# A four-layer transformer on one core: a repeating slot schedule replaced by one place for every operation of every batch

## What is computed

```python
x = x + tanh(g_xattn[0]) * xattn0(layernorm(x), ctx)   # 16 heads of 64, causal mask, softmax
x = x + tanh(g_ffn[0])   * ffn0(layernorm(x))          # ternary weights, 8-bit rows, silu gate
x = x + tanh(g_xattn[1]) * xattn1(layernorm(x), ctx)   # 16 heads of 8, mask
x = x + tanh(g_ffn[1])   * moe(layernorm(x))           # 8 experts, top 2, capacity 269 rows
x = x + tanh(g_xattn[2]) * xattn2(layernorm(x), ctx)   # one head, padding mask
x = x + tanh(g_ffn[2])   * ffn2(layernorm(x))          # gelu, layernorm inside, ternary weights
x = x + tanh(g_xattn[3]) * xattn3(layernorm(x), ctx)   # 16 heads of 8, biases
x = x + tanh(g_ffn[3])   * ffn3(layernorm(x))          # rmsnorm, relu squared, ternary weights
```

## Time and profile before

| | us |
|---|---|
| median of 3 runs | 485.5 (485.41 to 485.64) |
| span of the profiled execution | 482.6 |
| what lies around the span (485.5 - 482.6) | 2.9 |
| PE busy in the span | 388.5 (81%) |
| DVE busy | 287.2 (60%) |
| ACT busy | 263.1 (55%) |
| POOL busy | 180.6 (37%) |

### The profile page before, as it was taken

How to read it: one execution, slowest core, us unless ns; L and a number is a source line. 1 busy time by engine, 2 the same in 40 slices (tenths; PEclk the granted TensorE clock), 3 DMA queues, 4 the chain that set the end, 5 groups by cost and what they waited for, 6 DMA issues and landing times.

```text
span 482.6 us, 9945 instructions
## 1 busy us (share of the span) xinstructions
PE 388.5 (81%) x3550; PEld 281.1 (58%) x3564; DVE 287.2 (60%) x859; ACT 263.1 (55%) x781; POOL 180.6 (37%) x294
## 2 busy tenths in 40 slices
PE   3866999999997898999962999427778999889633
PEld 0645777767876665665541899315555666665522
DVE  3151575688687878665562121643546566898884
ACT  3234757676675778877631433422464766555532
POOL 3186334333424311355363000388726442221120
PEclk9597999999999999999985899855699999999955
DMA  8990000000000030000003241111000000000001
GB/s 338 394 381 6 1 2 1 1 2 2 2 1 1 1 133 1 1 13 18 20 22 93 59 130 36 45 33 27 7 0 1 3 1 1 2 2 3 3 0 43
DMA packets 7135, 22.11 MB, mean 46 GB/s; under 512 B 1215, under 2 KB 3503, under 8 KB 6575
## 3 DMA queue, kind: packets, MB, share of 16 engines
q1 hardware_dynamic: 6063, 19.38, 11.1%
q0 software_dynamic: 1024, 2.10, 1.5%
HBM read 14.60 MB, written 6.88 MB: 44 GB/s over the span
## 4 chain that ended last, share of the span: by engine, by line
PE 61%; ACT 11%; POOL 9%; DVE 7%; issue 7%; DMA 3%; SPq 0%; POOLq 0%; another core or an unknown queue 0%; DVEq 0%; ACTq 0%
PE bank L839 6%; PE bank L908 6%; PE bank L866 5%; ACT prob L565 5%; PE bank L1031 4%; PE bank L1022 3%; POOL moe_rows L488 3%; PE bank L822 3%; PE bank L854 3%; PE bank L903 3%; PE bank L917 3%; PE bank L810 3%; DVE mx L1236 3%; PE bank L888 2%; PE bank L975 2%
## 5 line engine op out<-in xcount | busy, mean ns | idle before, releaser
L565 ACT ACTIVATE prob<-bank,mx 128x128 f32<-128x128 f32 x256 | 82.3, 384 | 23.4 <-DVE mx L1236 23.2
L1236 DVE TENSOR_REDUCE mx<-bank 128x4 f32<-128x512 f32 x96 | 63.9, 682 | 41.0 <-PE bank L839 21.5
L468 POOL TENSOR_TENSOR prob<-prob,rden 128x512 f32<-128x512 f32 x32 | 33.2, 1039 | 69.2 <-DVE rden L1258 69.2
L550 ACT ACTIVATE probT<-bank 128x512 f32<-128x512 f32 x64 | 39.5, 617 | 29.9 <-PE bank L866 29.8
L866 PE MATMUL bank<-pack,prob 128*128 128x128 f32 x256 | 41.5, 286 | 7.6 <-POOL prob L468 4.6
L443 POOL TENSOR_TENSOR rstd<-rstd,minus_half 128x1 f32<-128x1 f32 x72 | 41.3, 573 | 6.0
L441 POOL TENSOR_SCALAR rstd<-mv 128x1 f32<-128x1 f32 x64 | 12.4, 193 | 83.0 <-DVE mv L1211 79.6
L866 PEld LDWEIGHTS bank<-pack,prob 128*128 128x128 f32 x256 | 28.7, 143 | 16.4 <-POOL prob L468 6.6
L488 POOL DMA_INDIRECT moe_rows<-yrows_d,row_of x16 | 16.0, 999 | 52.2 <-DMA yrows_d<-o_n 48.3
L462 POOL TENSOR_SCALAR xn<-pack,mv,rstd 128x128 f32<-128x128 f32 x32 | 25.9, 811 | 5.9 <-POOL rstd L443 5.4
L565 ACT ACTIVATION_READ_ACCUMULATOR prob<-bank,mx 128x1 f32 x128 | 27.9, 218 | 0.0
(11 more groups left out here) (233 smaller groups left out, 965.2 us busy)
## 6 DMA issues: line engine op xcount, KB each, us to landing
yrows_d<-moe_rows SPq DMA_DIRECT2D x2, 1510.0 KB, 21.2
pack<-pack_d SPq DMA_DIRECT2D x1, 2112.0 KB, 15.7
expert<-experts_d SPq DMA_DIRECT2D x4, 514.0 KB, 8.5
pack<-experts_d SPq DMA_DIRECT2D x4, 514.0 KB, 5.1
pack<-pack_d SPq DMA_DIRECT2D x1, 2048.0 KB, 10.3
xrows_d<-moe_rows SPq DMA_DIRECT2D x1, 1080.0 KB, 21.0
moe_rows<-xrows_d SPq DMA_DIRECT2D x8, 135.0 KB, 3.0
yrows_d<-o_n SPq DMA_DIRECT2D x8, 135.0 KB, 1.8
```

Of the source, the lines that this page charges most:

```text
L468: pool.tensor_tensor(part, part, r.to_broadcast([P, GH, P]), ALU.mult).then_inc(E[A0]["norm"].sem, 1)
L550: act.activation(dst, src, ACT.Identity if kw else ACT.Copy, **kw).then_inc(E[layer][name].sem, 1)
L565: act.activation(prob[:, g % 2, P * j:P * j + P], bank[S_BANK[g % 2]][:, P * j:P * j + P], ACT.Exp, bias=mx[:, g % 2, j:j + 1], **kw).then ...
L1236: dve.tensor_reduce(out, bank[S_BANK[g % 2]][:, :].rearrange("p (h t) -> p h t", h=GH), AX.X, ALU.max, negate=True).then_inc(E[layer]["max ...
```

## The change

`PLAN`, `LAG`, `steps_of` and `turns` go. `walk` takes a table in which each operation has eight numbers, one for each batch, and emits the operations of an engine by rising number; an operation that gives way between its instructions comes back `TURN` = 0.203 later. The numbers set the order within an engine, and nothing else; no engine looks at a clock. The one-off pieces have a number each and stand between two operations instead of between two steps. Tiles, banks and the operations themselves stay.

```diff
-def walk(eng, plan, stages, before={}, after={}, run=lambda layer, fn, it, *args: fn(it, *args)):
...
+def walk(stages, once=(), run=lambda layer, fn, it, *args: fn(it, *args)):
+
+    queue = []
+    for layer, entries in stages.items():
+        for b in range(B):
+            for fn, *args, places in entries:
+                if places[b] is not None:
+                    queue.append((places[b], len(queue), run, (layer, fn, Item(b, b), *args)))
+    for at, fn in once:
+        queue.append((at, len(queue), fn, ()))
+    while queue:
+        at, n, begin, args = head = min(queue, key=lambda entry: entry[0:2])
+        queue.remove(head)
+        rest = begin(*args)
+        if rest is not None:
+            if next(rest, stages) is not stages:
+                queue.append((at + TURN, n, lambda rest=rest: rest, ()))
...
-                    [(2, norm0, 0), (2, norm0, 1), (2, norm0, 2), (2, norm0, 3), (0, rs, A0)],
...
+                    (rs, A0, (-25.083, 23.918, 32.313, 57.517, 62.269, 77.402, 78.694, 125.511)),
...
-            walk(pool, PLAN, stages, before={(A2, 0): first_fetches}, after={(A0, 1): masks})
+            walk(stages, [(26.8, masks), (295.1, first_fetches)])
...
-                    [None, (3, resid, A0), None, None, (0, ln_stats, A0), (2, recip0, 3)],
...
+                    (ln_stats, A0, (-26.07, -23.462, 30.345, 46.548, 52.895, 72.757, 81.829, 113.251)),
```

More of the change, by code:

```diff
@@ L74, in at @@
         return self.per * item.b + (self.base + (self.per if j is None else j))
[L77 to L92, removed]
-def walk(eng, plan, stages, before={}, after={}, run=lambda layer, fn, it, *args: fn(it, *args)):
[L101 to L137, removed]
-            else:
-                with eng.Fori(0, passes) as i:
-                    for s in range(first, first + 2):
-                        single(layer, s, i)
@@ L1208, in ln_stats @@
                     wait(dve, BEFORE[layer], "resid", it)
+                wait(dve, layer, "rs", it.back(2))
                 do = chain(layer, "ln", it)
@@ L1370, in hid2_stats @@
                 wait(dve, F2, "gelu", it)
+                wait(dve, F2, "rs_hid", it.back(2))
                 do = chain(F2, "hid", it)
@@ L1586, in _ @@
-                    [],
-                    [None, (3, top_of, A3, 2), (5, resid, A3), (3, top_of, A3, 3)]],
-                F3: [
-                    [(1, ln_stats, F3), (1, quant3)],
-                    [(1, scale3), (2, square3)],
-                    [(4, resid_q, F3)],
-                    [(2, hq3)]],
-            }
+                    (ln_stats, A3, (356.677, 366.333, 371.607, 381.448, 386.526, 406.731, 416.843, 418.865)),
+                    (top_of, A3, 0, (366.37, 377.241, 387.238, 401.674, 410.087, 421.174, 428.949, 441.079)),
@@ new lines, in _ @@
+                    (norm, A3, (386.212, 399.541, 409.551, 420.938, 428.257, 440.48, 446.765, 455.111)),
+                    (resid, A3, (392.192, 405.442, 412.74, 422.329, 438.102, 444.03, 452.279, 461.816))],
+                F3: [
+                    (ln_stats, F3, (397.823, 408.928, 416.34, 422.362, 438.937, 444.43, 454.6, 462.132)),
+                    (quant3, (400.934, 411.942, 419.954, 423.774, 440.39, 444.78, 457.293, 462.579)),
+                    (scale3, (402.079, 412.292, 420.579, 431.854, 440.985, 446.372, 461.447, 466.518)),
+                    (square3, (417.994, 423.58, 436.454, 444.384, 450.66, 460.591, 463.058, 486.293)),
+                    (hq3, (420.48, 427.568, 437.856, 445.984, 454.49, 461.621, 466.989, 488.923)),
+                    (resid_q, F3, (431.17, 441.4, 448.13, 457.405, 462.574, 487.761, 492.452, 513.089))]}
```

376 lines of the change are left out of this document (207 added, 169 removed).

## The result

The changed kernel takes 459.75 us (median of 4 runs, 458.76 to 460.71) beside 485.46 before: ratio 0.948, 95% interval 0.9456 to 0.9504, 25.7 us less. The prediction had 469.0 and a range of 462 to 482. The direction was right and the size was not. The span of the profiled execution is 456.9, 25.7 less than before as well.

What follows compares the result with a forecast made beforehand. PE was taken to bound the first part and 365.6 to 405.7 us, DVE and PE equally full after, a serial chain ending it. Terms 7.0 + 2.5 + 1.5 + 4.0 + 0 + 1.5 = 16.5 gave 469.0 us, range 462 to 482.

Steps and rivals of the forecast that it cites:

- Start, 7.0: Start of A0: masks and `norm0` begin earlier (5.7 us) and PE's low clock shortens (1.3); 7.0 us, bounds 3 to 8.
- one move of `ln_stats`: Start, DVE: `ln_stats` of batch 1 directly follows batch 0's, so POOL's `rs` and masks come earlier; within the 7.0 us.
- First part and the end of A1, 2.5 + 1.5: A0 to A1: fewer PE waits, 2.5 us; last `norm` of A1 closer to its `pv`, 1.5 us, bounds 0 and 2.
- the counted wait: A0, batches 2 to 7: PE's 0.37 us wait for the transposition's copy goes, 6 x 0.37 = 2.2 us.
- The upper bound of 8: First part: bounds on the 2.5 us term, 8 us gained or 3 lost.
- Third part up to A3, 4.0: Up to A3: A3 starts earlier (1.7), earlier gelu (3.0), less POOL's 0.7; 4.0 us, bounds 7 gained, 2 lost.
- the late start of batch 0: Third part: batch 0's first row maximum of A2 comes later; if that reaches F2, 2 us lost.
- A3 and F3 in full flow 0, tail 1.5: A3/F3: both engines about 88% full, 0, bounds 3 either way; tail: shorter wait of last `y`, 1.5, 4 gained, 1 lost.
- the wait of 5.09 us: Tail: A3's last `y` waits for `resid_q` of F3's batch 3 to empty bank 7; predicted under 4 us.
- more than I find: Rival: half of PE's first-part idle time and upper bounds at clock and A3 also come; 460.8 us, chance 0.12.
- Slower, through copies behind exponentials: Rival: in A0, A1, A3 PE waits for ACT's copies behind 1.51 us exponential groups; 505 us, chance 0.08.
- Only the start pays: Rival: new waits where engines are full give back the other terms; 478.5 us, 475 to 482, chance 0.25.

Runs made afterwards that it cites:

- the swap: `resid_q` of F3's batch 3 on DVE, ahead of `scale3` and `square3` in the before order: 482.91 beside 485.53; put back later in the changed kernel: 461.54 us.
- mixed kernels: Changed kernel's bodies and waits, one kernel's order up to a moment, the other's behind: new up to MOE 470.97 us, old up to MOE 472.76.

## Why the prediction was right and wrong

**Start, 7.0: right.** Measured 7.2 (new order up to the first `y`). `norm0` came 5.5 earlier (5.7 said). In the profile the clock gave 2.48 instead of 1.3, as the rule of the Trainium skill had it; in five other profiles of this start it gave less, 0.9 in the one shown above. That the total fits so well is in part luck: the profile has 8.8 (5.5, 2.5 and 0.8 of idle time), and 1.6 of it is not in the time. I gave the whole to one move of `ln_stats`; alone it earns 4.4 to 4.8.

**First part and the end of A1, 2.5 + 1.5: too small.** Measured 6.4 together (470.97 against 477.38). At the end of A1 `norm` came 1.8 us closer to its `pv`, as argued. In the body the counted wait went in full (2.2), but it was one of five kinds, and I set the other four to nothing. PE's idle time fell by 5.6. The upper bound of 8 was wide enough.

**Third part up to A3, 4.0: the lead came, but it is not earned there.** By the profiles the first sum on DVE starts 1.8 us earlier than the lead, since the keys no longer stand ahead of it. From that sum to F2's first transposition the new order takes 30.7 us instead of 27.8, the late start of batch 0 that stood in the bounds. From there to A3's first transposition it takes 17.7 or 20.0 instead of 24.1 (last section). That is 1.8 - 2.9 + 6.4 or 4.1 = 5.3 or 3.0, near the 4.0. But with the old order behind it this part earned 0.6 us (470.97 to 470.41), within the noise, and the earlier start of A3's products was paid back in A3: most of the lead was work put off. So I counted as won what only the order behind A3's start turns into time.

**A3 and F3 in full flow 0, tail 1.5: this is the step that failed.** The two terms had 1.5 together. Measured from A3's first transposition to the end: 5.7 + 0.4 = 6.1 by the two profiles; by the times, the new order from that transposition on earns 8.7 alone, and the part of it behind the sixth `y` 4.3 to 5.5. I read that both engines are about 88% full from 365.6 to 452.6 and concluded that a new order has nothing to win there. The reading holds for the second of the two stretches only: in the first DVE works 24.95 of 40.10 us, 62%. And the conclusion does not follow where an engine is full: which work it does first decides when the last batch comes to DVE, and PE was idle for 7.5 of the 16.3 us from the sixth `y` to the last. Products that nobody waited for (the next batch's `pv` and second scores, F3's `up`) stood ahead of `y`. They now fill that hole; with five of the eight `y` put back behind such products, the last `y` comes 7.2 us later. And of the wait of 5.09 us I looked only at the two steps right ahead of its releaser, worth 1.8, and asked which of them remains due. That was about right for the swap (0.5 and 1.1 net by the profiles, 2.6 and 1.8 by the medians), but the whole of DVE's order ahead of it had moved.

**The rivals.** The case nearest to the result was "more than I find", 460.8, with a chance of 0.12; the measured 459.75 lies below that too. Its first item (half of PE's idle time) nearly came true (7.8 us idle instead of 13.4), the clock did in the profile (2.48 us), its third (7 us up to A3) in part, and it had nothing for A3's body either, so that its nearness is in part luck. *Slower, through copies behind exponentials* did not happen: PE's waits for exponentials in A0 and A1 sum to 0.9 us after (4.3 before). *Only the start pays* had 0.25, on the argument that new waits open where engines are full. The mixed kernels show that this danger is real where the engines' orders do not match (the output products moved on PE alone), and not where all are laid together.

## What to carry to other kernels

A full engine bounds a stretch only for a fixed set of work in it: look at where that engine is idle later, and for work in the full stretch that could be done there. With in-order engines an order is one thing across all of them: moving output products forward on PE alone cost 3 to 7 us; the same direction, as part of an order in which all engines moved, stands in the stretch of A3 that is 5.7 us shorter. Nor is a lead at a milestone a gain: ask what was put off behind it. So price a new order by the stretches from one milestone to the next, not by the single wait, and when a row shows five kinds of waits of one engine, ask of each whether the change reaches it.

## What was not expected of the hardware

The stretch from F2's first transposition to that of A3 took 24.0 to 24.3 us in every profile with the old order there (23.2 in the kernel whose order changes at the end of the stretch). With the new order it took 17.6 to 17.7 in four profiles and 19.9 to 20.2 in six, though all ten have the same order in it. They differ in when the clock rises: at most 2.2 us behind F2's first transposition in the four (in two of them ahead of it, with one more fall of 3.4 us later), 11.6 to 12.2 us behind it in the six. After, and the run that is new up to A3's fourth `y`:

```profile
328.30:335.00 6.70, 4.74 (x21) 3.08 (x21) 4.58 (x18) 4.67 (x10) 4.40 (x9) 0.84 0.03 7
```

```profile
328.80:338.00 9.20, 8.10 (x26) 5.27 (x26) 5.08 (x21) 5.75 (x14) 5.89 (x13) 0.50 0.04 8
```

The product `up` of batch 1 takes 1.03 us in the first run (at 335.5 us) and 1.91 in the second (at 337.4). So about 2.3 us of this kernel's time hang on whether the clock rises at 331 us or some 10 us later in a loosely filled stretch; the changed kernel's own runs lie at 458.8 and 459.0, and at 460.5 and 460.7. That these pairs are the two cases was not shown.

Another part of the spread is the start: PE's first product that needs the second half of the value weights starts between 21.8 and 24.4 us in twenty profiles, and what follows moves with it. Its cause was not found: the two weight loads that land nearest to it do so at 18.9 to 19.5 and 23.4 to 24.3 us, a spread of under 1 us each.
